# An LSTM and feed-forward kernel on one core: the order of its first loads and casts

## What is computed

```python
xW = jnp.einsum('ntd,dg->ntg', x, Wx) + b
def step(carry, xw_t):
    prev_h, prev_c = carry
    a = xw_t + prev_h @ Wh
    ...
    next_c = f * prev_c + i * g
    next_h = o * jnp.tanh(next_c)
    return ((next_h, next_c), next_h)
...
h = jnp.concatenate([x, -x], axis=-1)
h = s0 * _conn_dense(k0, h)
h = jax.nn.relu(h) * 2
h = s1 * _conn_dense(k1, h)
h = jax.nn.relu(h) * 2
h = s2 * _conn_dense(k2, h)
...
x = x + _L0_ffn_ref(_L0_cond_ref(x, cond_1024, L0_cond_Wx, L0_cond_Wh, L0_cond_b), L0_ffn_k0, L0_ffn_k1, L0_ffn_k2, L0_ffn_s0, L0_ffn_s1, L0_ffn_s2)
```

## Time and profile before

| what | value |
|---|---|
| median of three runs | 277.6 us |
| lowest, highest | 277.39, 278.2 us |
| the profiled execution's own time | 277.77 us |
| its span | 276.0 us |
| TensorE matmul busy | 272.2 us, 99% |
| VectorE busy | 203.5 us, 74% |
| ScalarE busy | 158.0 us, 57% |
| GpSimd busy | 2.2 us, 1% |

### The profile page before, as it was taken

One profiled execution on the slowest core, in us unless ns is written; L12 is line 12 of the kernel. 1 busy time (PEld: TensorE's weight loads), 2 busy tenths in 40 slices (PEclk: granted clock), 3 DMA queues, 4 the chain that ended last, 5 costly groups with the idle time before them and its releaser, 6 DMA issues.

```text
span 276.0 us, 8792 instructions
## 1 busy us (share of the span) xinstructions
PE 272.2 (99%) x3616; PEld 224.0 (81%) x3616; DVE 203.5 (74%) x751; ACT 158.0 (57%) x482; POOL 2.2 (1%) x10
## 2 busy tenths in 40 slices
PE   8999999999999999999999999999999999999996
PEld 5887888888999998999999999999999996444443
DVE  3778888878888888888888888888887876532213
ACT  5689787878566656655555566555665554411100
POOL 0200000000000000000000000000000000000000
DMA  6970000000000000000000000000000000010002
GB/s 221 362 298 1 4 2 0 2 4 2 2 2 0 5 21 21 2 2 4 21 23 2 1 21 21 2 2 23 22 3 0 21 23 2 0 38 2 0 0 76
DMA packets 5191, 8.72 MB, mean 32 GB/s; under 512 B 672, under 2 KB 3488, under 8 KB 5024
## 3 DMA queue, kind: packets, MB, share of 16 engines
q1 hardware_dynamic: 4864, 7.64, 7.8%
q10 hardware_dynamic: 288, 0.52, 0.5%
HBM read 6.07 MB, written 2.10 MB: 30 GB/s over the span
## 4 chain that ended last, share of the span: by engine, by line
PE 97%; DMA 1%; DVE 0%; DVEq 0%; issue 0%
PE WK L465 50%; PE WK L448 14%; PE G L427 11%; PE ACC L481 10%; PE G L418 9%; DMA x<-in_x 1%; PE G L448 1%; PE ACC L448 1%; PE G L481 0%; DVE xs L715 0%; DVE x L662 0%; DVEq L237 0%
## 5 line engine op out<-in xcount | busy, mean ns | idle before, releaser
L465 PE MATMUL WK<-h,k 128*128 128x256 f16 (+1 forms) x992 | 124.2, 276 | 0.0
L465 PEld LDWEIGHTS WK<-h,k 128*128 128x128 fp8e5 x992 | 94.2, 98 | 13.4
L609 ACT ACTIVATE tT<-aT 128x128 f32<-128x128 f32 x126 | 39.0, 310 | 56.4 <-DVE aT L759 55.2
L655 DVE SCALAR_TENSOR_TENSOR h<-WK,h 128x256 f16<-128x256 f32 (+1 forms) x105 | 42.6, 439 | 24.7 <-ACT h L574 24.7
L759 DVE TENSOR_REDUCE aT<-G 128x128 f32<-128x256 f32 x128 | 48.1, 417 | 7.7 <-PE G L427 6.1
L574 ACT ACTIVATE h<-WK 128x256 f16<-128x256 f32 (+1 forms) x104 | 36.3, 387 | 28.8 <-PE WK L465 28.8
L556 ACT ACTIVATE G<-xw 128x256 f32<-128x256 f32 x126 | 46.6, 370 | 0.0
L448 PE MATMUL WK<-xs,wxs 128*128 128x512 f32 x168 | 42.5, 400 | 0.0
L427 PE MATMUL G<-h,w 128*128 128x64 f16 x1008 | 39.5, 192 | 0.0
L418 PEld LDWEIGHTS G<-h,w 128*128 128x128 f16 x1008 | 32.9, 96 | 5.8 <-DVE h L776 4.4
L448 PEld LDWEIGHTS WK<-xs,wxs 128*128 128x128 f32 x168 | 30.4, 188 | 5.9
(11 more groups left out here) (66 smaller groups left out, 132.8 us busy)
## 6 DMA issues: line engine op xcount, KB each, us to landing
x<-in_x SPq DMA_DIRECT2D x3, 512.0 KB, 7.8
out_y<-x SPq DMA_DIRECT2D x12, 128.0 KB, 1.8
xw<-in_wh SPq DMA_DIRECT2D x4, 256.0 KB, 4.8
k<-in_k SPq DMA_DIRECT2D x1, 1024.0 KB, 9.6
x<-in_x ACTq DMA_DIRECT2D x2, 256.0 KB, 3.8
xw<-in_wx SPq DMA_DIRECT2D x4, 128.0 KB, 3.9
xw<-in_wx SPq DMA_DIRECT2D x2, 256.0 KB, 5.1
k<-in_k SPq DMA_DIRECT2D x1, 512.0 KB, 6.9
```

Of the source, the lines that this page charges most:

```text
L465: ins = eng.matmul(layer_src(tile), w, rhs, start=a == 0, stop=last)
L609: eng.activation(tT[:, B * j0:B * j1], aT[:, j0:j1].rearrange("p j b -> p (j b)"), ACT.Tanh, scale=half_gain0 if t == 0 else half_gain).th ...
L655: eng.scalar_tensor_tensor(layer_dst(tile, 1), layer_src(tile), 0.0, layer_dst(tile, 0), ALU.max, ALU.subtract).then_inc(lo_made[tile[0]])
```

## The change

- Wx's first group is cut in two: (k 0, j 0) and (k 0, j 1), 64 KB each, so there are seven groups, and their numbers move up by one from the second on.
- x's k = 0 half of the first quarter is loaded as columns 0 to 255 on ScalarE's queue and columns 256 to 511 on SyncE's, behind Wx's first group. VectorE casts the first piece, ScalarE the second. TensorE and `x_lo(0, 0)` wait for both.
- x's k = 1 half is issued by ScalarE behind the tanh instead of ahead of it.
- Wx's last two groups are issued by ScalarE, behind its cast of x's second piece and ahead of `wx_hi(1)`, instead of by SyncE among and behind the loads of Wh.
- TensorE takes, for each half k, all three matmuls of a tile before the next tile's, instead of alternating two tiles.
- The matmuls on zeros are 15 instead of 16.

```diff
-WARM = 16
+WARM = 15
-WX_GROUPS = ((0, 1, 0, 2), (0, 1, 2, 4), (1, 2, 0, 2), (1, 2, 2, 4), (0, 2, 4, 6), (0, 2, 6, 8))
+WX_GROUPS = ((0, 1, 0, 1), (0, 1, 1, 2), (0, 1, 2, 4), (1, 2, 0, 2), (1, 2, 2, 4), (0, 2, 4, 6), (0, 2, 6, 8))
...
             if i == 0 and k == 0:
                 e.wait_ge(xh0, 1)
+                e.wait_ge(xh0_end, 1)
...
         def _(eng):
             e = Seen(eng)
-            for g in range(4):
-                load_wx(g)
+            load_wx(eng, 0)
+            eng.dma_start(x[:, 0, 0, 256:512], x_d[:, 0, 0, 256:512]).then_inc(dx0_end, 16)
+            load_wx(eng, 1)
+            load_wx(eng, 2)
+            load_wx(eng, 3)
+            load_wx(eng, 4)
             eng.dma_start(small[:, :], small_d[:, :]).then_inc(dsmall, 16)
             for g in range(4):
                 eng.dma_start(wh[:, 2 * g:2 * g + 2], wh_d[:, 2 * g:2 * g + 2]).then_inc(dwh[g], 16)
-                if g == 0:
-                    load_wx(4)
-            load_wx(5)
...
             for a0 in (0, 3):
                 for j0 in (0, 2):
-                    for a in range(a0, a0 + 3):
-                        for j in (j0, j0 + 1):
+                    for j in (j0, j0 + 1):
+                        for a in range(a0, a0 + 3):
                             matmul(("x", 0, j), a)
...
-            eng.dma_start(x[:, 0, 0], x_d[:, 0, 0]).then_inc(dx0[0], 16)
-            eng.dma_start(x[:, 0, 1], x_d[:, 0, 1]).then_inc(dx0[1], 16)
+            eng.dma_start(x[:, 0, 0, 0:256], x_d[:, 0, 0, 0:256]).then_inc(dx0[0], 16)
             e.wait_ge(zeroed, 1)
             eng.activation(warm[:, :], zero[:, 0:NJ], ACT.Tanh)
+            eng.dma_start(x[:, 0, 1], x_d[:, 0, 1]).then_inc(dx0[1], 16)
             wx_hi(0)
+            e.wait_ge(dx0_end, 16)
+            eng.activation(xs[:, 0, 0, 0, 256:512], x[:, 0, 0, 256:512], ACT.Copy).then_inc(xh0_end)
+            load_wx(eng, 5)
+            load_wx(eng, 6)
             wx_hi(1)
+            wx_hi(2)
             x_hi(0, 1)
-            wx_hi(2)
             wx_hi(3)
             wx_hi(4)
+            wx_hi(5)
             for j in range(4):
                 x_empty(("x", 0, j))
-            wx_hi(5)
+            wx_hi(6)
...
             e.wait_ge(dx0[0], 16)
-            eng.tensor_copy(xs[:, 0, 0, 0, :], x[:, 0, 0]).then_inc(xh0)
+            eng.tensor_copy(xs[:, 0, 0, 0, 0:256], x[:, 0, 0, 0:256]).then_inc(xh0)
             wx_lo(0)
             x_lo(0, 0)
             wx_lo(1)
+            wx_lo(2)
             x_lo(0, 1)
-            wx_lo(2)
             wx_lo(3)
+            wx_lo(4)
...
-            wx_lo(4)
+            wx_lo(5)
...
-            wx_lo(5)
+            wx_lo(6)
```

More of the change, by code:

```diff
@@ L309, in lstm_ffn @@
         dx0 = [sem(f"dx0_{k}") for k in range(2)]
+        dx0_end = sem("dx0_end")
         dx = [sem(f"dx{i}") for i in range(1, 4)]
@@ L314, in lstm_ffn @@
         wxh, wxl, whi, wlo, xh, xl = (sem(n) for n in ("wxh", "wxl", "whi", "wlo", "xh", "xl"))
-        xh0, xh1 = sem("xh0"), sem("xh1")
+        xh0, xh0_end, xh1 = sem("xh0"), sem("xh0_end"), sem("xh1")
         zeroed, maxed, max_all, scaled, biased, signed, hz_hi, hz_lo = (
@@ L369, in wx_part, with load_wx @@
             return v[:, k0:k1, j0:j1].rearrange("p k j c -> p k (j c)")
+        def load_wx(eng, g):
+            eng.dma_start(wx_part(wx, g), wx_part(wx_d, g)).then_inc(dwx[g], 16)
         block = ctx.enter_context(nc.Block())
@@ L375, in _ @@
             e = Seen(eng)
-            def load_wx(g):
-                eng.dma_start(wx_part(wx, g), wx_part(wx_d, g)).then_inc(dwx[g], 16)
-            for g in range(4):
-                load_wx(g)
+            load_wx(eng, 0)
[4 more added lines that the diff above has]
+            load_wx(eng, 4)
             eng.dma_start(small[:, :], small_d[:, :]).then_inc(dsmall, 16)
```

## The result

The changed kernel takes 280.48 us in the median of six runs (280.25 to 280.94), the kernel before 277.71 (277.28 to 278.2): a ratio of 1.0102, 95% interval 1.0087 to 1.0116, or 2.8 us more. The forecast was 277.4, in a range of 276.8 to 278.2.

A forecast was written before the change was run, and what follows sets the result against it. The bound was the first x matmul's moment plus TensorE's list. Ramp-limited gain -0.34 plus 0.1 for ScalarE's issues gave -0.24: 277.77 to 277.53, or 277.4 for the median, in a range of 276.8 to 278.2 us.

The forecast's parts named there:

- The bound: Whole kernel: its time is the moment of the first x matmul plus TensorE's fixed list.
- I take 3.7: Load of x's second piece: lands at 3.7 us, bounded by 3.5 and 4.2, so the first x matmul starts at 4.26.
- Rival B: First x loads: k = 1 half issued during the table load, pieces land near 4.1; 277.6 to 277.9 us, chance 0.2.
- The ramp: First x matmuls: clock still rises at about 5.3, so starting 0.51 us earlier gains only 0.34 us.
- Rival C: x matmuls from 4.26 on: clock stays low longer, each us past 5.34 costing 0.5 us; slower, chance 0.1.
- What is queued behind the two issues on ScalarE: Wx's two issues, some 1.2 us, delay `wx_hi(1)` and TensorE's fourth matmul: charged 0.1 us, bounds 0 and 0.4.
- At most 256 KB more stand ahead of it, at 335 GB/s: Wh's loads on SyncE: at most 0.78 us later, a wait of 0.4 us at step 0 at worst; taken as zero.
- the slack of 0.62: Before step 0: seeds end at 18.81, step 0 starts at 19.44; 0.24 of it goes with TensorE's earlier arrival.
- The warning about small loads: First 64 KB loads: 0.47 us each by the skill page, start up to 0.47 later; left out of the sum.

The follow-up runs named there:

- e11: The changed kernel, unchanged, run once more for a second trace: 281.13 us.
- e8: The changed kernel with 16 matmuls on zeros, Wx's last groups on SyncE, x's k = 1 half issued behind ScalarE's cast of the second piece: 279.79 us.
- e13: The kernel before with Wx's k = 1 groups, tiles 0 to 3, in four 64 KB loads instead of two of 128 KB: 278.12 us.
- e9: The kernel before with 8 matmuls on zeros instead of 16: 279.03 us (ratio 1.0061).
- e7: The kernel before with x's first half in two loads on two queues, cast by two engines: 278.38 us (ratio 1.0036).
- e3: The changed kernel with Wx's last two groups issued by SyncE again: 279.44 us (ratio 1.0055).
- e4: The changed kernel with Wx's last two groups issued by SyncE again and 19 matmuls on zeros: 278.78 us (ratio 1.0041).
- e5: The kernel before with only Wx's last two groups moved to ScalarE's queue, between its first two casts of Wx: 279.14 us (ratio 1.0041).
- e1: The changed kernel with 19 matmuls on zeros instead of 15: 280.24 us (ratio 1.0089).
- e15: The changed kernel with 19 matmuls on zeros, Wx's last groups on SyncE, Wx's k = 1 groups in one load, small inputs on ScalarE's queue: 278.83 us.
- e10: The kernel before, unchanged, run once more for a second trace: 277.61 us.
- e14: The kernel before with x's k = 1 half in two loads of 128 KB on the same queue: 277.98 us (ratio 1.0014).
- e6: The kernel before with Wx's first group cut in two 64 KB loads and the new order of matmuls: 278.17 us (ratio 1.0006).
- e12: The changed kernel with 16 matmuls on zeros, Wx's last groups and x's k = 1 half on SyncE: 278.95 us (ratio 1.0045).

## Why the prediction was wrong, point by point

**The bound** was right: the moment of the first x matmul plus TensorE's list, with step 0 as the place where the rest would show. The list from step 0 on takes as long as before, to 0.2 us.

**"I take 3.7"** for the landing of x's second piece, with 4.2 as the upper end. It landed just before 4.52, and 4.76 in e11. The value was right for a load without competition (landed before 3.73 in e8); the condition failed, since the k = 1 half was issued at 1.24, 0.07 us into the table load. Rival B had this at 0.2. The upper end failed as well: I took it from today's landing of the whole half, though the piece now stood on the other queue behind Wx's load and shared the engines with a half of 256 KB.

**The ramp, "nothing moves that moment by itself".** It does move. With 16 matmuls on zeros and an idle stretch no longer than before's, the rise came before 4.9 in e13 and near 6.9 in e8; in the changed kernel near 9.6 in one trace and before 6 in the other (e11). With fewer matmuls on zeros (e9: 1.4 us), or with an idle stretch before the x matmuls (three of e7's ten runs), the time grows in part of the executions or most. That this is a later rise is seen in the traces of e3 (near 8.9) and of the changed kernel; why it comes in one execution and not in the next, no run shows. Rival C had the mechanism and its price per us right, at a chance of 0.1, and argued against itself with an idle stretch of 0.1 that B's condition turned into 0.9. I priced B and C apart, and in these runs B's late piece brought C with it. The Trainium skill, "TensorE: Matmul & The Clock Gate", Part 1, says that the moment differs between runs; the traces agree, with the first six matmuls in 2.90 us and in 2.20 (e11) in the same kernel.

**What is queued behind the two issues on ScalarE.** The issues took 1.28 us, as forecast. The fourth matmul was not pushed in the first trace, where the lower clock hid it (its cast ends at 6.17, it starts at 6.50), and by 0.2 in e11 (6.46). The failed step is the other half of the same edit: I priced how long the issues hold ScalarE, and put at nothing what the move does to the loads themselves. Wx's tiles 4 and 5 were issued 1.0 us later, behind Wh's second load and on a queue that shares the engines with the rest of Wh, and were cast 3.7 us later (11.79 for 8.08). e3 and e4 issue them as late, but on SyncE ahead of Wh's second load, and cast them at 9.39 and 9.69: 2.1 to 2.4 us are the price of that place. e5 has this part of the change alone: 1.1 us. I had weighed what the move does to the loads of Wh, and not what it does to Wx's.

**"At most 256 KB more stand ahead of it, at 335 GB/s".** The rate was taken as given. It fell to 242, and the last reduction of Wh's parts began at 14.2 (13.06 + 1.87 - 0.69) instead of 10.74, 3.5 us later where the bound was 0.78. Part of that is VectorE's order: the reductions stand behind `wx_lo(5)`, which waited for the late group. With that the seeds came at 21.76, and the slack of 0.62 was gone.

**How the loss adds up.** It doesn't add up by parts: the late clock, the late group and the late Wh each set step 0 to within some tenths of 21.8, and taking away the first leaves 280.24 (e1), the late group 279.44 (e3), both 278.78 (e4). Of the last 1.05 us e4's trace shows 0.78 by step 0 (20.22 for 19.44): 0.15 is the later start (4.92), most of the rest the slower traffic behind it (the wait for Wx's last group at 13.92). No run takes the traffic's share away by itself: e15 restored the traffic and had a later start.

**The warning about small loads.** The Trainium skill, "DMA: Bandwidth & Descriptors", section "Bandwidth", gives it for loads under 64 KB, from figures of loads that GpSimd issued. By the rows the first 64 KB landed by 2.93 here and by 3.30 in e11, where the 128 KB of before landed by 4.01 and by 3.61 (e10), so the early cost that I estimated from it isn't there. What was paid came afterwards, and e14, with a load more and pieces as small as e7's, didn't pay it.

## What to carry to other kernels

A load that moves to another engine's queue changes two things: what its issue holds up there, and when it lands. Issued at the same moment, the same load landed over 2 us later on ScalarE's queue, with one load of Wh more ahead of it and the others beside it. Price the landing, and then whoever stands in order behind the one that waits for it. Keep TensorE busy up to the first real matmul: a stretch of idling there can cost, in part of the executions, far more than its own length, by the time at half rate behind it. When several loads feed one list, look for the next limit before pricing the removal of one.

## What the runs showed of the hardware

- ScalarE's sequencer issues a load during the table load: 1.24, in a table load from 1.17 to 2.45.
- A 256 KB load issued on ScalarE at 3.74 to 4.77 landed 4.4 to 7.6 us later (x in e8; Wx in e5, e1, e11), one issued on SyncE at 4.00 to 4.97 within 4.6 to 5.4 (Wx in e6, e7, e3, e4, e12). The first loads, at 0.72, landed within 2.2 to 3.5. "DMA: Bandwidth & Descriptors" of the Trainium skill, section "Issuing engines are not separate DMA queues", says that loads of all engines run on the same DMA engines and interleave. The changed kernel's trace agrees from 7.5 us on (98 and 117 packets of the two queues in 1 us); from 4.6 to 7.4 it shows SyncE's queue alone.
- Traffic behind a start with more loads was lower for some 5 us: 356 GB/s with four loads ahead of Wh, 327 to 340 with five (310 in e5), 278 and 290 with six, mostly 236 to 259 with seven.
- The granted clock reads 1.00 in stretches in which matmuls are 0.427 apart; the level has to be read from the starts (of the first six x matmuls in the changed kernel, for one).
